# Gated y and B of an attention stage turned by VectorE's 32x32 block transposes and a store and load through DRAM, instead of TensorE transposes

## What is computed

```python
proj = x @ W_in.T                          # 512 -> xp 512, z 512, B 256, C 256, dt 16
dt = softplus(dt_low @ dt_W.T + dt_b)      # 16 heads
dA = dt * A;  dAcs = cumsum(dA) in chunks of 64 tokens
scores = einsum('bcihn,bcjhn->bcijh', C, B) * exp(dAcs_i - dAcs_j) * causal * dt
y_intra = einsum('bcijh,bcjhp->bcihp', scores, xp)
chunk_state = einsum('bckhn,bckhp->bchnp', B, dt * decay_to_end * xp)
y = y_intra + C @ h_states * exp(dAcs) + xp * D_param
y = y / rms(y) * norm_w * silu(z)          # the gated y
out = y @ W_out.T
```

## Time and profile before

| what | value |
|---|---|
| median of 3 runs | 2917.99 us (2916.21 to 2919.55) |
| the profiled execution | 2926.86 us, its span 2925.1 us |
| TensorE busy | 2769.8 us, 95% of the span |
| VectorE, ScalarE, GpSimd busy | 70%, 59%, 50% |
| granted TensorE clock, mean | 0.988 |
| chain that ended last | TensorE 89%, VectorE 4%, issue 4% |

### The profile page before, as it was taken

The page is one execution under the profiler, slowest core; times in us unless marked ns, Lnnn a source line. Parts: engine busy times, 40 slices in busy tenths (PEclk is TensorE's granted clock), DMA queues, the critical chain, the costliest instruction groups (busy, mean ns, idle before and its releaser), DMA issues.

```text
span 2925.1 us, 135112 instructions
## 1 busy us (share of the span) xinstructions
PE 2769.8 (95%) x59836; PEld 2237.4 (76%) x59836; DVE 2053.4 (70%) x2871; ACT 1715.0 (59%) x3424; POOL 1463.4 (50%) x2319
## 2 busy tenths in 40 slices
PE   8999999999999999999999999999677787899998
PEld 7888888888888888888888888887566676455554
DVE  6777777777777777777777777777444443788998
ACT  5666566566666666656656656665333333666674
POOL 4666666666667667666666666666110000111111
PEclk9999999999999999999999999999899998899999
DMA  4222222222222222222222222222644443578776
GB/s 154 78 73 69 74 78 76 73 78 77 72 79 74 72 82 73 73 77 74 75 75 78 74 72 79 76 73 58 215 132 136 110 123 119 178 222 269 234 228 195
DMA packets 262711, 316.37 MB, mean 108 GB/s; under 512 B 28000, under 2 KB 184032, under 8 KB 260464
## 3 DMA queue, kind: packets, MB, share of 16 engines
q1 hardware_dynamic: 252176, 297.55, 33.7%
q10 hardware_dynamic: 9952, 10.17, 1.1%
HBM read 194.31 MB, written 113.31 MB: 105 GB/s over the span
## 4 chain that ended last, share of the span: by engine, by line
PE 89%; DVE 4%; issue 4%; DMA 1%; SPq 1%; POOL 1%; ACT 0%; ACTq 0%; DVEq 0%; POOLq 0%
PE a_proj L991 41%; PE a_mix L991 12%; PE s_ps L1714 6%; PE g_pick_ps L1465 6%; PE a_scan L1105 5%; PE s_ps L1735 4%; DVE g_picked L1394 3%; PE s_ps L1730 3%; PE a_scan L1082 3%; PE a_scan L1069 2%; PE g_acc_ps L1489 2%; PE a_mix L1057 2%; PE a_misc L1049 1%; PE a_misc L1123 1%; DMA part_dram<-res 1%
## 5 line engine op out<-in xcount | busy, mean ns | idle before, releaser
L991 PE MATMUL a_proj<-wdh,xTh 128*128 128x512 f32 x1024 | 421.2, 411 | 5.5 <-issue 3.7
L991 PE MATMUL a_proj<-wdh,xTl 128*128 128x512 f32 x1024 | 402.4, 393 | 0.3 <-issue 0.3
L991 PE MATMUL a_proj<-wdl,xTh 128*128 128x512 f32 x1024 | 400.0, 391 | 1.7 <-issue 1.7
L823 DVE COPY_PREDICATED scan_in<-mask,a_scan 64x512 f32<-64x512 uint32 x512 | 382.4, 747 | 16.1
L1671 ACT COPY s_stage<-s_ps 128x1024 f32<-128x1024 f32 x256 | 279.2, 1147 | 150.9 <-PE s_ps L1714 142.4
L464 POOL TENSOR_TENSOR dx<-xs,d_row 64x512 f32<-64x512 f32 x256 | 331.4, 1294 | 15.1
L472 POOL TENSOR_TENSOR yv<-yt,dx 128x512 f32<-128x512 f32 x128 | 189.0, 1476 | 293.2 <-DVE yt L863 293.2
L639 ACT ACTIVATE scan_in<-CT,hsel 64x128 f32<-64x128 f32 x1024 | 326.2, 388 | 4.8
L603 ACT ACTIVATE raw<-a_proj,rs 128x272 f32<-128x272 f32 x128 | 62.5, 488 | 427.4 <-PE a_proj L991 427.4
L1394 DVE COPY g_picked<-g_pick_ps 128x1024 f32<-128x1024 f32 x128 | 156.7, 1224 | 218.4 <-PE g_pick_ps L1465 218.4
L1691 DVE STREAM_TRANSPOSE s_turned<-s_stage 128x2048 f32<-128x2048 f32 x128 | 294.4, 2302 | 9.8 <-ACT s_stage L1671 9.8
(11 more groups left out here) (152 smaller groups left out, 7275.3 us busy)
## 6 DMA issues: line engine op xcount, KB each, us to landing
x<-in_x_dram SPq DMA_DIRECT2D x128, 256.0 KB, 2.7
xn_dram<-xn SPq DMA_DIRECT2D x128, 256.0 KB, 2.4
part_dram<-res SPq DMA_DIRECT2D x128, 256.0 KB, 2.5
g_xn<-xn_dram SPq DMA_DIRECT2D x512, 64.0 KB, 2.3
s_part<-part_dram SPq DMA_DIRECT2D x128, 256.0 KB, 4.1
out_dram<-s_out SPq DMA_DIRECT2D x128, 256.0 KB, 3.8
xr<-in_xT_dram SPq DMA_DIRECT2D x126, 256.0 KB, 2.9
s_inner<-inner_dram SPq DMA_DIRECT2D x32, 512.0 KB, 4.1
```

Of the source, the lines that this page charges most:

```text
L823: nc.vector.copy_predicated(dst, mask[rows_, :].unsqueeze(1).unsqueeze(1).to_broadcast([CH, 4, 2, CH]), src).then_inc(mt_cp, 1)
L991: last = nc.tensor.matmul(out, lhs[a], rhs[c], start=(k == 0 and n == 0), stop=(k == nk - 1 and n == 2))
```

## The change

The twelve TensorE transposes of a step go (only the last tile keeps its four). Instead VectorE turns 32x32 blocks (a block transpose leaves each block in its place, so the 4 x 4 grid of blocks still has to be turned), writes them to the tile `blocks`, SyncE stores that to DRAM, waits, and loads it back in four DMAs, one for each group of 32 partitions, which puts the blocks where a full transpose would have them. There are two such trips in a step: the **even trip** (`move_even(s)`) takes B of both tiles of step s and the gated y of tile n1, 512 KB each way, to the tile `even`; the **odd trip** (`move_odd(s)`) takes the gated y of tile n2+1, 256 KB each way, to the tile `odd`. ScalarE's `copy_bT` and `hi_yz` and VectorE's `lo_yz` read `even` and `odd` in SBUF instead of PSUM; `yg`, the pair that project_out reads, is doubled.

The places in the programs move as well: `hi_yz(n1)` now ends ScalarE's step s (before it was `hi_yz(n2)` of the next step), `lo_yz(n1)` stands on VectorE behind `mask_scores(n1+1)`, `hi_yz(n2+1)` behind `square(n2+1)`, and `lo_yz(n2+1)` behind `mask_scores(n1)`. Three more SBUF tiles and the end of the used SBUF (`AT_END`) only make room. The diff's core:

```diff
@@ -117,6 +120,9 @@
     BT = sb("BT", [P, 2, P])
+    blocks = sb("blocks", [P, 4, 2 * KI, GRP], at=AT_LATE)
+    even = sb("even", [P, 4, 2 * KI, GRP], at=AT_LATE + 4096)
+    odd = sb("odd", [P, 4, KI, GRP], at=AT_LATE + 8192)
     gs = sb("gs", [P, NG, 2 * HD])
@@ -332,8 +345,20 @@
         if n < NT - 1:
-            return [y[:] for y in yg]
+            return [y[:] for y in yg[n % 2]]
         return [y[:] for y in yl]
+
+    def features(n):
+
+        return (odd[:] if n % 2 else even[:, :, 0:KI, :]).rearrange("p b k t -> p k b t")
+
+    def even_part(s):
+
+        return slice(0 if valid(s - 1) else KI, 2 * KI if valid(s) else KI)
+
+    def odd_steps(s):
+
+        return max(0, s - 1)
@@ -346,6 +371,31 @@
             sync.dma_start(xr_place(s)[:, 2 * i:2 * i + 2, :], io["xT"][s][:, 2 * i:2 * i + 2, :]).then_inc(xr_in[s % 2], 16)
+
+        def move_even(s):
+            part = even_part(s)
+            cols = slice(GRP * part.start, GRP * part.stop)
+            if valid(s):
+                sync.wait_ge(b_turned, s + 1)
+            if valid(s - 1):
+                sync.wait_ge(y_turned, 2 * s - 1)
+            sync.dma_start(keep["even"][s, :, :, cols], blocks[:, :, part, :].rearrange("p g k t -> p g (k t)")).then_inc(even_out, 16)
+            sync.wait_ge(even_out, 16 * (s + 1))
+            wait(sync, yg_lo, 2 * s - 3)
+            if valid(s - 1):
+                wait(sync, bT_cp, 2 * s)
+            for g in range(4):
+                sync.dma_start(even[GRP * g:GRP * g + GRP, :, part, :].rearrange("p b k t -> p b (k t)"),
+                               even_rows[s, g][:, :, cols]).then_inc(even_in, 16)
+
+        def move_odd(s):
+            sync.wait_ge(y_turned, 2 * s - 2)
+            sync.dma_start(keep["odd"][s], blocks[:, :, 0:KI, :].rearrange("p g k t -> p g (k t)")).then_inc(odd_out, 16)
+            sync.wait_ge(odd_out, 16 * odd_steps(s))
+            wait(sync, yg_lo, 2 * s - 4)
+            for g in range(4):
+                sync.dma_start(odd[GRP * g:GRP * g + GRP, :, :, :].rearrange("p b k t -> p b (k t)"),
+                               odd_rows[s, g]).then_inc(odd_in, 16)
@@ -416,6 +466,8 @@
                 load_rsb(s)
+            if valid(s - 2) and s < NST + 1:
+                move_odd(s)
             if valid(s + 1):
@@ -423,6 +475,8 @@
                 load_x(2 * (s + 2))
+            if s < NST + 1:
+                move_even(s)
             if valid(s + 1):
@@ -600,11 +654,14 @@
             wait(act, st_ps, 2 * (n - 3))
+            wait(act, b_turned, n // 2 - 1)
             nc.scalar.activation(raw[:, n % 4, :], proj[n % 2][:, 0:C_C], ACT.Copy, scale=inv(n)).then_inc(bdt_cp, 1)
         def copy_bT(n):
-            act.wait_ge(bT_ps, n + 1)
-            nc.scalar.copy(BT[:], misc[:, 0:HALF].rearrange("p (f t) -> p f t", f=2)).then_inc(bT_cp, 1)
+            act.wait_ge(even_in, 64 * (n // 2 + 1))
+            wait(act, sc_ps, 4 * n)
+            part = KI + 2 * (n % 2)
+            nc.scalar.copy(BT[:].rearrange("p f (b t) -> p b f t", t=GRP), even[:, :, part:part + 2, :]).then_inc(bT_cp, 1)
@@ -646,11 +703,15 @@
         def hi_yz(n):
-            act.wait_ge(yzT_ps, n + 1)
             if n == NT - 1:
+                act.wait_ge(yzT_ps, 1)
                 for i in range(2):
                     act.wait_ge(xn_out[i], 16 * NST)
-            nc.scalar.copy(gated(n)[0], turned(n)[:].rearrange("p (k t) -> p k t", k=KI)).then_inc(yg_hi, 1)
+                nc.scalar.copy(gated(n)[0], turned(n)[:].rearrange("p (k t) -> p k t", k=KI)).then_inc(yg_hi, 1)
+            else:
+                act.wait_ge((even_in, odd_in)[n % 2], 64 * (n // 2 + 2 - n % 2))
+                wait(act, o_ps, n - 1)
+                nc.scalar.copy(gated(n)[0].rearrange("p k (b t) -> p k b t", t=GRP), features(n)).then_inc(yg_hi, 1)
@@ -696,8 +757,6 @@
                 bias_exp(s)
-            if valid(s - 2):
-                hi_yz(n2)
             if s == NST + 1:
@@ -712,6 +771,8 @@
                 square(n2 + 1, 1)
+            if valid(s - 2) and s < NST + 1:
+                hi_yz(n2 + 1)
             if s == NST + 1:
@@ -732,9 +793,8 @@
                 out_hi()
-            if valid(s - 2):
+            if s == NST + 1:
                 hi_yz(n2 + 1)
-            if s == NST + 1:
                 gather["copy_perm"](act, 0, 1)
@@ -749,6 +809,7 @@
                 square(n1, 0)
+                hi_yz(n1)
@@ -867,14 +928,36 @@
             dve.wait_ge(z_cp, n + 1)
-            wait(dve, yzT_ps, n - 1)
+            wait(dve, y_turned, n - 1)
             nc.vector.tensor_tensor(yz[:, n % 2, :], yv[:], sz[:, n % 4, :], ALU.mult).then_inc(yz_cp, 1)
+
+        def turn_yz(n):
+
+            s = n // 2 + 1 + n % 2
+            wait(dve, even_out, 16 * s)
+            wait(dve, odd_out, 16 * odd_steps(s - n % 2))
+            dve.wait_ge(yz_cp, n + 1)
+            nc.vector.transpose(blocks[:, :, 0:KI, :], yz[:, n % 2, :].rearrange("p (k g l) -> p g k l", k=KI, g=4)).then_inc(y_turned, 1)
+
+        def turn_b(s):
+
+            wait(dve, even_out, 16 * s)
+            wait(dve, odd_out, 16 * odd_steps(s))
+            dve.wait_ge(scaled, 2 * s + 2)
+            for i in range(2):
+                last = nc.vector.transpose(blocks[:, :, KI + 2 * i:KI + 2 * i + 2, :],
+                                           raw[:, (2 * s + i) % 4, C_B:C_DT].rearrange("p (f g l) -> p g f l", f=2, g=4))
+            last.then_inc(b_turned, 1)
...
             hi, lo = gated(n)
-            nc.vector.tensor_tensor(lo, turned(n)[:].rearrange("p (k t) -> p k t", k=KI), hi.bitcast(F32),
-                                    ALU.subtract).then_inc(yg_lo, 1)
+            if n == NT - 1:
+                nc.vector.tensor_tensor(lo, turned(n)[:].rearrange("p (k t) -> p k t", k=KI), hi.bitcast(F32),
+                                        ALU.subtract).then_inc(yg_lo, 1)
+            else:
+                hi, lo = [y.rearrange("p k (b t) -> p k b t", t=GRP) for y in (hi, lo)]
+                nc.vector.tensor_tensor(lo, features(n), hi.bitcast(F32), ALU.subtract).then_inc(yg_lo, 1)
@@ -938,6 +1021,8 @@
                 gate(n2 + 1)
+            if valid(s - 2) and s < NST + 1:
+                turn_yz(n2 + 1)
             if s == 0:
@@ -946,11 +1031,11 @@
                 finish_stats(2 * (s + 1))
-            if valid(s - 2):
-                lo_yz(n2)
             if valid(s - 1):
...
                 mask_scores(n1)
+            if valid(s - 2) and s < NST + 1:
+                lo_yz(n2 + 1)
             if s == NST + 1:
@@ -964,15 +1049,18 @@
                 expand_c(n1 + 1)
+            if valid(s):
+                turn_b(s)
+            if valid(s - 1):
                 gate(n1)
+                turn_yz(n1)
             if valid(s + 1):
...
                 finish_stats(2 * (s + 1) + 1)
-            if valid(s - 2) and s < NST + 1:
-                lo_yz(n2 + 1)
             if valid(s - 1):
...
                 mask_scores(n1 + 1)
+                lo_yz(n1)
             if s == 1:
@@ -1088,6 +1166,8 @@
             pe.wait_ge(yg_lo, n + 1)
+            if n < NT - 1:
+                wait(pe, res_cp, n)
             for k in range(KI):
@@ -1108,7 +1188,7 @@
             pe.wait_ge(dA_ready, s + 1)
-            wait(pe, bT_cp, 2 * s)
+            wait(pe, mg_ready, s)
             for j in range(0, P, 32):
@@ -1163,19 +1243,13 @@
                 project_bdt(n0 + 1)
-            if valid(s - 1):
-                transpose_b(n1)
             if valid(s):
                 project_x(n0)
-            if valid(s - 2):
-                transpose_yz(n2)
             if valid(s - 1):
...
                 project_z(n0)
-            if valid(s - 1):
-                transpose_b(n1 + 1)
             if s == NST:
@@ -1197,8 +1271,6 @@
                 gather["pick"](pe, 0, 1)
-            if valid(s - 2) and s < NST + 1:
-                transpose_yz(n2 + 1)
             if valid(s - 1):
```

30 lines of the change are left out of this document (16 added, 14 removed).

## The result

The changed kernel takes 3098.22 us (median of 4 runs, 3096.76 to 3100.77) against 2917.64 for the kernel before in the same runs: a ratio of 1.0619, 95% interval 1.0601 to 1.0638. That is 180.6 us more, where 135 were forecast.

The account below looks back on a forecast made before the run. TensorE set the pace before; afterwards a ring through VectorE, POOL and the even DRAM trip was to bind at 33.53 us a step instead of 31.38. Over 63 steps that adds 135 us to 2918: 3053 us, range 2950 to 3130.

Parts of the forecast that it names:

- the case that had 0.73: The even trip alone on the ring of instructions closing once per step, total between 2945 and 3115 us; chance 0.73.
- What TensorE loses: Transposes removed from TensorE: 0.52 us per gated y, 0.22 per B, two of each, 1.48 us a step.
- The transposes of VectorE: Block transposes added on VectorE: 0.70 us per gated y, 0.43 per B, 2.27 us a step.
- The ring: VectorE, POOL, the even DRAM trip, ScalarE and back to VectorE's picks, once per step: 32.84 us, 33.53 with POOL's turn-taking.
- Leg (d): The even trip through DRAM: store 3.3 us, 1.38 until the last load's issue, load 2.6; 7.28 in all.
- Leg (c): VectorE's gate(n1), 0.69 us, and turn_yz(n1), 0.70 us: 1.39 us.
- (g): Five hand-overs between engines of 0.04 us each: 0.2 us a step.
- The collision: lo_yz, now with two SBUF inputs, takes turns with POOL: the second half of dx(n1) waits 0.69 us.
- (b): From VectorE's lo_x through POOL's work up to gate(n1): 15.04 us, 15.73 with POOL's wait for lo_yz.
- The number: 33.53 less 31.38 is 2.15 us a step, over 63 steps 135 us, added to 2918: 3053 us.
- These waits cost nothing on top; they are the same 2.15 us: TensorE's waits ahead of sums (0.92 us of room) and project_bdt were taken to add nothing to the step's 2.15 us.
- The rivals: Trip hidden, 2823 to 2912 us if a gain, chance 0.13; odd trip binds too, beyond 0.9 us of room, chance 0.14.

Follow-up runs that it names:

- e1: The changed kernel with both casts (hi_yz and lo_yz, of both tiles) put back to their old places, half a step later: 2991.96 us, ratio 1.0229.
- e3: The changed kernel with the store of the even trip made twice, the second behind a wait for the first: 3294.06 us (one run).
- e6: The kernel before with only lo_yz's operand changed, to the unturned yz in SBUF in place of the turned one in PSUM: 2923.82 us, ratio 1.0019.
- e10: The kernel before with only the change's DRAM tensors and its size of the runtime's scratch: 2921.46 us, ratio 1.0005.
- e11: The kernel before with the DMAs of both trips added, whose data nobody reads or waits for: 2916.24 us, ratio 1.0012.

## Why the prediction was right, and where it was short

The sign, the mechanism and the range held: 3098 us lies inside 2950 to 3130, in the case that had 0.73. By its steps:

- **What TensorE loses**: right. B's removal gave 0.47 us a step (0.44 forecast), one gated y's 0.5 (0.52).
- **The transposes of VectorE**: 712 ns for a gated y and 434 for 256 columns, 0.70 and 0.43 forecast.
- **The ring**: right leg by leg, and e1 and e3 show that it binds. Leg (d) has a mean of 7.51 us for 7.28. The store lands at 2.6 us in most steps, under my 3.3, but at up to 4.85 in others; the load takes 3.10 to its use, my upper end. The two errors nearly cancel. Of the estimate from the Trainium skill, "DMA: Bandwidth & Descriptors", section "Anatomy of one DMA" (3.2 and 2.3 us, by a fit for DMAs of another issuing path), both parts are off: the store was mostly shorter (2.64 in the median) and the load longer (3.10). Leg (c), 1.67, holds two of the hand-overs of (g). The step is 33.63 in the median, 33.53 forecast, and 33.96 in the mean.
- **The collision**: right in kind, and its size right in part by luck. e6 shows it alone. (b) is 15.67 for 15.73 forecast and 15.05 before, but the 0.69 us were to fall on the second half of dx(n1), and that grew by 0.31 in the mean: dx(n1) is 3.2 us long in 35 of the 64 steps and about 2.65 in the others. The way up to dA lost 0.2; the remaining 0.5 lies behind dx, 0.35 of it at `yv`, which waits 0.14 and runs 1.45 us for 1.28, and 0.12 at the first instruction of inv_rms. Those nobody had forecast.
- **The number**: mis-sized by the subtraction. I took one step of before, 31.38 us; the mean over 52 is 31.62. The means differ by 2.31 us, and 63 times that is 146, as the loop shows (144.7). Both terms of 33.53 - 31.38 were too small, by 0.4 and by 0.24: a step from one place of the trace, and landings that are at times much longer than their median.
- **What was left out**: the end of the stage, 34.9 us at the passage, 17.6 net in this pair and some 20 by the groups of kernels above. The step that failed is the factor of the sum, 63 equal steps with nothing for the last round. In that round the odd trip's place in SyncE's queue is behind the next stage's weights. The order of the queue showed it. Of the last stage's 11.5 us more nothing is explained; e10 excludes the placing in DRAM, and e11 the traffic in the loop (448.0 us). There is an order in it that no experiment took up: the five kernels whose gated y stays with TensorE take 448.0 to 452.4 us there, the eight that send all or half of it through DRAM 452.6 to 462.1, with one trace of each.
- **"These waits cost nothing on top; they are the same 2.15 us"**, of TensorE ahead of `sums` and project_bdt: true only as long as the trip is on the ring. They belong to a second ring with 0.92 us of room, which the change overdraws too, and which left e1 at 1.023.
- **The rivals**: the odd trip stays off the ring. ScalarE waited for `odd` 8.5 us in all between 200 and 2000 us, for `even` 80.7. It was closer than the 0.9 us of room make it look: the odd store took 3.6 us in the median where the rival's sum had 2.4, the loads 1.9 for 2.4, and the longest of the 15 waits for `odd` is 1.2 us.

## What to carry to other kernels

In a pipelined loop, write down each ring that closes in one step, and its room, before moving an operation to another engine: a trip through DRAM of some 7.5 us is free where its result is due a step later (B, and the odd gated y) and costs all that exceeds the ring's room where the instructions behind its reader lead to the next step. Moving only what TensorE's own ring pays for and the others have room for gave 0.985, moving all of it 1.062. And read the loop's last round apart: there the loads ahead in the queue are those of the next stage.
